# A graph network on one core: both counting sorts made bucket by bucket, source ranks in 40 written-out groups, node loads behind the fill

## The reference

```
h = features @ W_layer.T + b_layer                       # layer 1
v = leaky_relu(a1[row] + a2[col]);  m = segment_max(v, row)
ev = exp(v - m[row])
out = segment_sum(ev / segment_sum(ev, row)[row] * h[col], row)
...
for l in range(3):                                       # layers after the router
    msg = relu(x[src] * (edge_attr @ edge_w + edge_b))
    for i in range(3):                                   # three edge types
        h = segment_sum(msg * (edge_type == i), dst) * inv_cnt[i]
        out = out + h @ weights[l, i]
    out = out + x @ roots[l] + biases[l]
    x = residual + relu(out)
```

## Time and profile before

| | |
|---|---|
| median of the runs | 5961.54 us |
| profiled execution, its own time | 5950.92 us |
| its span | 5949.1 us |
| busy in the span: PE, DVE, ACT, POOL | 75%, 71%, 38%, 69% |
| mean granted TensorE clock | 0.904 |

### The profile page before, as it was taken

How to read it: one execution, slowest core, us unless ns; L and a number is a source line. 1 busy time by engine, 2 the same in 40 slices (tenths; PEclk the granted TensorE clock), 3 DMA queues, 4 the chain that set the end, 5 groups by cost and what they waited for, 6 DMA issues and landing times.

```text
span 5949.1 us, 89553 instructions
## 1 busy us (share of the span) xinstructions
PE 4487.4 (75%) x25082; PEld 2797.4 (47%) x25082; DVE 4196.2 (71%) x9654; ACT 2286.6 (38%) x5880; POOL 4087.5 (69%) x4202
## 2 busy tenths in 40 slices
PE   6459987899888876777777767777776777777787
PEld 2135544666666644444444434444444444444455
DVE  8789986777777654666766757777675777777734
ACT  0038875555555523333333323333332223232321
POOL 1467777777777777777777757777776777777700
PEclk9579998888898888999999989999999999999979
DMA  5011111434333313444444434444444444445400
GB/s 149 19 40 29 29 26 37 108 107 107 106 102 101 93 35 111 135 135 129 133 133 131 134 104 139 139 138 139 139 139 117 137 139 138 140 138 140 137 25 22
DMA packets 445005, 624.93 MB, mean 105 GB/s; under 512 B 97099, under 2 KB 330261, under 8 KB 444564
## 3 DMA queue, kind: packets, MB, share of 16 engines
q0 software_dynamic: 187648, 457.52, 27.7%
q1 hardware_dynamic: 250164, 159.14, 9.5%
q10 hardware_dynamic: 6754, 2.96, 0.2%
HBM read 556.32 MB, written 62.94 MB: 104 GB/s over the span
## 4 chain that ended last, share of the span: by engine, by line
PE 25%; DVE 14%; issue 11%; POOL 10%; ACT 2%; DVEq 2%; DMA 1%; POOLq 0%; ACTq 0%; SPq 0%
PE banks L1173 13%; DVE acc_mem L1692 6%; POOL sort_mem L623 6%; DVE z_mem L1835 5%; PE banks L1203 4%; POOL recB_d L581 3%; PE banks L1161 2%; PE banks L1106 1%; PE banks L1116 1%; DMA sort_mem<-x_d,x_mem 1%; DVEq L1681 1%; DVEq L1692 1%; ACT z_mem L809 1%; PE banks L1158 1%; PE banks L1193 1%
## 5 line engine op out<-in xcount | busy, mean ns | idle before, releaser
L623 POOL DMA_INDIRECT sort_mem<-x_d,x_mem x2568 | 2454.3, 956 | 877.7 <-issue 764.3
L1173 PE MATMUL banks<-z_mem 128*128 128x257 f32 x5136 | 1567.7, 430 | 903.9 <-DVE acc_mem L1692 766.8
L1173 PEld LDWEIGHTS banks<-z_mem 128*128 128x128 f32 x5136 | 850.5, 199 | 1601.3 <-ACT z_mem L809 718.4
L1692 DVE TENSOR_TENSOR acc_mem<-acc_mem,banks 128x257 f32 x2568 | 1081.8, 421 | 556.0 <-PE banks L1173 383.0
L809 ACT ACTIVATE z_mem<-z_mem 128x512 f32<-128x512 f32 x1284 | 768.8, 628 | 1375.6 <-DVE z_mem L1835 1375.6
L1835 DVE TENSOR_TENSOR z_mem<-banks,sort_mem 128x512 f32<-128x512 f32 x1284 | 825.4, 685 | 412.3 <-PE banks L1161 301.6
L581 POOL DMA_INDIRECT recB_d<-acc_mem,sort_mem x680 | 708.6, 1042 | 410.6 <-DVE sort_mem L1423 205.4
L590 POOL DMA_INDIRECT acc_mem<-h_d,xnt_mem x808 | 798.3, 988 | 246.1 <-issue 235.5
L1049 PE MATMUL banks<-acc_mem,xnt_mem 128*128 128x257 f32 x1616 | 579.3, 483 | 44.0 <-DVE acc_mem L1635 41.8
L1635 DVE SCALAR_TENSOR_TENSOR acc_mem<-acc_mem,z_mem,banks 128x257 f32 x808 | 386.7, 479 | 114.8 <-PE banks L1049 100.4
L1161 PE MATMUL banks<-z_mem,x_mem 32*128 32x256 f32 x5136 | 422.1, 404 | 0.0
(11 more groups left out here) (355 smaller groups left out, 5714.1 us busy)
## 6 DMA issues: line engine op xcount, KB each, us to landing
x_mem<-recB_d SPq DMA_DIRECT2D x642, 68.0 KB
sort_mem<-x_d,x_mem POOLq DMA_INDIRECT x2568
x_mem<-at_d SPq DMA_DIRECT2D x428, 64.0 KB
at_d<-x_mem SPq DMA_DIRECT2D x214, 64.0 KB
acc_mem<-h_d,xnt_mem POOLq DMA_INDIRECT x808, 2.8
x_mem<-x_d SPq DMA_DIRECT2D x100, 128.0 KB, 2.5
acc_mem<-in_edge_attr SPq DMA_DIRECT2D x40, 312.5 KB
recB_d<-acc_mem SPq DMA_DIRECT2D x3, 3672.0 KB, 26.1
```

The costliest lines, as they stand in the source:

```text
L623: pool.indirect_dma_start(out=xg[h % XG][:, k, :], out_offset=None, in_=x_ds[l % 2], in_offset=bass.IndirectOffsetOnAxis(ap=reci[h][:, k, ...
L1173: m.matmul(bank[5 + tile % 2][:, :AC], oneh[:, Q % 2, k, :], msg[:, Q % 2, k, :], start=True, stop=True)\
L1692: v.tensor_tensor(a_, a_, bank_[:, :AC], ALU.add).then_inc(flushed, 1)
```

## The change

Four parts. (1) `count` makes one mask of all 800 columns for each bucket (`tensor_scalar` with a constant) and PE adds its two halves of 400 columns to row b of two banks, so that the counts come out as [bucket, column] with no transposes. The masks lie in `held`, 25 slots; sort B goes round them three times, sort A's stay for its ranks. (2) Sort A's ranks are made in 40 groups of 20 columns, written out, with the product of group q ahead of the reduce of q-1; product and matrices are now bucket-major, so the reduce reads them with a step of 20 elements. Late body 3 moves ahead of them. Sort A's base is not turned before it is stored: 25 rows of 800. (3) On SP the load of x and first weights moves from ahead of the fill to behind the loads of late body 1, and POOL makes the fill record and `pick` first, record memsets last. (4) DVE splits only the target ids before sort B; the source's part (`split_ids`) and the items (`make_items`) come later. ACT stores sort B's base before it makes records.

```diff
+        GROUPS_A = EC // 20
+        def mask_slot(b):
+            return held[:EP, b % BKT_A, :]
+        def hot_A(q):
+            return held[:, :, q * 20:(q + 1) * 20]
+        def in_buckets(m_):
+            return m_[:EP, :20 * BKT_A].rearrange("p (b c) -> p b c", b=BKT_A)
+        FILL_MADE, GRID_MADE, ALL_MADE = 5, 13, 15 + len(late_recs)
...
@@ SP
-            x_rows = t["x"][0:(NT - 1) * P, :].rearrange("(t p) d -> p t d", p=P)
-            sp.wait_ge(S("x_zeroed"), 1)
-            sp.dma_start(x_sb[:, 0:NT - 1, :], x_rows).then_inc(S("x_loaded"), 16)
...
+            def load_nodes():
+                x_rows = t["x"][0:(NT - 1) * P, :].rearrange("(t p) d -> p t d", p=P)
+                sp.wait_ge(S("x_zeroed"), 1)
+                sp.dma_start(x_sb[:, 0:NT - 1, :], x_rows).then_inc(S("x_loaded"), 16)
...
-            sp.wait_ge(S("fill_ready"), 1)
+            sp.wait_ge(S("p_const"), FILL_MADE)
...
                 if i + 2 < BODIES:
                     load_attr(i + 2)
+                if i == 1:
+                    load_nodes()
...
@@ ACT
+            store_base_B()
+            act.wait_ge(S("p_const"), ALL_MADE)
             act.wait_ge(S("items_ready"), 1)
-            for i in range(2):
+            for i in range(4):
                 make_records(i)
-            store_base(SORT_B)
-            for i in range(2, 4):
-                make_records(i)
-            store_base(SORT_A)
-            act.dma_start(held[EP:, :], baseA_d).then_inc(S("held_rows"), 16)
+            store_base_A()
...
@@ PE, count
-                            m.matmul(bank[half][:4 * n, :cols * nb], pick[:, ds((i * 4 + k) * -1 + 79, 4 * n)],
...
+                for b in range(nb):
+                    pe.wait_ge(S("onehot"), before + b + 1)
+                    for half in range(2):
+                        last = m.matmul(bank[half][:nb, :EC // 2], pick[:, 79 - b:79 - b + nb],
+                                        mask_slot(b)[:, half * (EC // 2):(half + 1) * (EC // 2)], start=b == 0, stop=b == nb - 1)
+                    last.then_inc(S("counted"), 1)
...
@@ PE, ranks
+            late_body(3)
             pe.wait_ge(S("held_rows"), 16)
+            for q in range(GROUPS_A):
+                if q >= 2:
+                    pe.wait_ge(S("rank_masked"), q - 1)
+                m.matmul(in_buckets(bank[q % 2]), tri_b[:, :EP], hot_A(q), start=True, stop=True).then_inc(S("ranked"), 1)
...
@@ DVE, count
+                for b in range(nb):
+                    if b >= BKT_A:
+                        dve.wait_ge(S("counted"), b - BKT_A + 1)
+                    v.tensor_scalar(mask_slot(b), s["key"], float(b), None, ALU.is_equal).then_inc(S("onehot"), 1)
+                if n_ == 0:
+                    make_items()
+                    dve.wait_ge(S("p_const"), GRID_MADE)
...
@@ DVE, ranks
+            def product_A(q):
+                dve.wait_ge(S("ranked"), q + 1)
+                if q >= 2:
+                    dve.wait_ge(S("rank_summed"), q - 1)
+                v.tensor_tensor(in_buckets(prod[q % 2]), in_buckets(bank[q % 2]), hot_A(q)[:EP], ALU.mult)\
+                    .then_inc(S("rank_masked"), 1)
+            def slots_A(q):
+                dve.wait_ge(S("rank_masked"), q + 1)
+                v.tensor_reduce(slotf[:, q * 20:(q + 1) * 20], in_buckets(prod[q % 2]).rearrange("p b c -> p c b"),
+                                X_AXIS, ALU.add).then_inc(S("rank_summed"), 1)
...
             count(SORT_B)
+            split_ids()
             late_body(0)
             late_body(1)
             count(SORT_A)
             late_body(2)
-            looped_from(dve, 0, SORT_A["bodies"] // 2, rank_A)
             late_body(3)
-            looped_from(dve, SORT_A["bodies"] // 2, SORT_A["bodies"], rank_A)
+            for q in range(GROUPS_A):
+                product_A(q)
+                if q:
+                    slots_A(q - 1)
```

More of the change, by code:

```diff
@@ L127, in looped @@
             body(n - 1)
-        def looped_from(eng, lo, hi, body):
-            body(lo)
-            with eng.Fori(lo + 1, hi - 1) as i:
-                body(i)
-            body(hi - 1)
         x_mem = sb("x_mem", [P, NT * D])
@@ L547, in _ @@
             g.memset(fill, 0.0).then_inc(S("p_const"), 1)
-            g.memset(erec, 0.0).then_inc(S("p_const"), 1)
-            for late in late_recs:
-                g.memset(late, 0.0).then_inc(S("p_const"), 1)
-            g.iota(addrB, pattern=[[1, EC]], base=P * TB - EP * EC, channel_multiplier=EC).then_inc(S("p_const"), 1)
+            g.memset(pick, 0.0).then_inc(S("p_const"), 1)
+            pool.wait_ge(S("p_const"), 2)
+            g.memset(pick[:, 79:80], 1.0).then_inc(S("p_const"), 1)
+            g.memset(fill.rearrange("p (t c) -> p t c", c=RW)[:, :, W_SEG:W_SEG + 1], -1.0).then_inc(S("p_const"), 1)
+            g.iota(fill.bitcast(INT32).rearrange("p (t c) -> p t c", c=RW)[:, :, W_SRC:W_SRC + 1], pattern=[[1, 8], [0, 1]],
+                   base=0, channel_multiplier=24).then_inc(S("p_const"), 1)
             g.iota(iota, pattern=[[1, P]], base=0, channel_multiplier=0,
@@ L873, in _ @@
             m = nc.tensor
-            pe.wait_ge(S("const_ready"), 1)
+            pe.wait_ge(S("p_const"), FILL_MADE)
             def count(s):
-                nb, cols, n_ = s["nb"], s["cols"], s["n"]
-                before = n_ * GROUPS_B
-                for half in range(2):
-                    n = s["bodies"] // 2
-                    def body(i):
-                        for k in range(4):
-                            q = (i + half * n) * 4 + k
-                            pe.wait_ge(S("onehot"), before + q + 1)
-                            if half == 0 and isinstance(i, int) and i == 0 and k == 0 and n_ == 1:
-                                pe.wait_ge(S("counts_read"), 1)
-                            m.matmul(bank[half][:4 * n, :cols * nb], pick[:, ds((i * 4 + k) * -1 + 79, 4 * n)],
-                                     hot(s, k, q)[:EP], start=isinstance(i, int) and i * 4 + k == 0,
-                                     stop=isinstance(i, int) and i * 4 + k == 4 * n - 1).then_inc(S("counted"), 1)
-                    looped(pe, n, body)
-                for half in range(2):
-                    pe.wait_ge(S("rows_copied"), n_ * 2 + half + 1)
-                    G = s["bodies"] * 2
-                    for c in range(cols):
-                        last = m.transpose(bank[2 + half][:nb, c * G:(c + 1) * G], prod[half][:G, c * nb:(c + 1) * nb],
-                                           ident[:G, :G])
-                    last.then_inc(S("counts_turned"), 1)
+                nb, n_ = s["nb"], s["n"]
+                before = n_ * BKT_B
+                if n_:
+                    pe.wait_ge(S("counts_read"), 1)
+                for b in range(nb):
[4 more added lines that the diff above has]
+                    last.then_inc(S("counted"), 1)
+                pe.wait_ge(S("const_ready"), 1)
                 pe.wait_ge(S("tiles_ready"), n_ + 1)
@@ L1262, in _ @@
             st.settle()
[L1263 to L1285 removed]
+            st.run(v.scalar_tensor_tensor(keyB, hi_i, float(R), rel_i, ALU.mult, ALU.add))
@@ new lines, in make_items, with split_ids @@
+            def make_items():
+                st.did(v.tensor_copy(itemB[:, 0, :].bitcast(INT32), src_i))
+                st.run(v.tensor_copy(itemB[:, 1, :], lo_i))
+                dve.sem_inc(S("items_ready"), 1)
+            def split_ids():
+                dve.wait_ge(S("p_const"), ALL_MADE)
+                st.did(v.tensor_single_scalar(hi_i, src_i, 7, ALU.logical_shift_right))
+                st.did(v.tensor_single_scalar(lo_i, src_i, 127, ALU.bitwise_and))
+                st.did(v.tensor_scalar(dstm, dst_i, float(-MID), None, ALU.add))
+                st.settle()
+                st.did(v.tensor_copy(keyA, hi_i))
+                st.did(v.tensor_scalar(segp, lo_i, 1.0, None, ALU.add))
+                st.did(v.tensor_copy(iota_h, iotaT[:, :TA]))
+                st.settle()
```

173 lines of the change are left out of this document (60 added, 113 removed).

## The result

The changed kernel takes 5877.19 us, the median of 4 runs (5873.36 to 5877.75), against 5962.59 of the kernel before beside it (4 runs, 5959.02 to 5966.57): 85.4 us less, a ratio of 0.9854 (95% interval 0.9839 to 0.987). The profiled execution takes 5877.75 with a span of 5875.9; that is 73.2 less than the earlier trace rows; the run of the kernel before that was profiled (5950.92) was 11.7 under the median of the others, and the part on the unchanged kernels says where.

A forecast was written before the change was run, and what follows sets the result against it. POOL was taken to wait for DVE's slot addresses until body 8, then run its own fixed row. Gains 3.7 + 45.3 + 2.1 + 19.8 + 0.8 + 7.9 + 12.3 = 91.9 took 5961.5 to 5869.6 us, range 5846 to 5904.

The forecast's parts named there:

- The mechanism: POOL waits for DVE until body 8's address at 427.94 us; that moves to 336, so the whole 91.9 us passes.
- Ids: DVE from first id split to sort B's first mask: three instructions, 2.15 us instead of 5.9, gain 3.7.
- Sort B's count: Sort B's masks on DVE and matmuls on PE: 29.7 us instead of 75.0, gain 45.3; bounds 27 and 50.7.
- The rival of a low clock throughout: PE stays at low clock in both counts, 50.7 and 17.4 us; gain 65.7, time 5896; chance 0.18.
- Source split hidden behind the base store: The put-off split_ids, some 3.1 us on DVE, is hidden in the 3.62 wait for sort B's base store.
- The fill ends by 60: On SP's queue the fill, issued from about 2.5 us, ends by 60, before the first scatter at 76.5.
- Sort A's count, tail: Sort A's masks and counts 12.2 us instead of 32.0, gain 19.8; its copies, tail and base parts gain 0.8.
- Base rows of sort A: DVE's 7.9 us wait for sort A's base rows is covered by a second late body; gain 7.9, or 6.7.
- Ranks: Sort A's ranks on DVE: 40 groups of 1.66 us, 67.4 instead of 79.7, gain 12.3.
- nothing extra: Rival: the ranks' stepped reads cost nothing, 14.4 us more gain, time 5855; chance 0.10.
- twice the extra: Rival: the ranks' stepped reads cost twice the extra, time 5884; chance 0.07.
- SP: Load of x and weights starts about 74 us, ends by about 97; late body 2's base rows, wanted about 105, stay unaffected.

The follow-up runs named there:

- the part on the unchanged kernels: Kernel before and changed kernel profiled again, unchanged; body 8's address to first gather took 591.1 and 614.5 before, 597.9, 600.2 and 609.7 changed.
- the added 18.7 us: Changed kernel plus 20 unused reduces of 500 f32 elements on DVE ahead of late body 4; median 5907.16 us.
- the further 16.9 and 25.6: Changed kernel with sort A's product in column pairs, 5885.90 us; with pairs, a third product buffer and ten unused PE matmuls before sort A's masks, 5871.27 us.

## Why the prediction was right

5870 was forecast, 5877.19 measured, inside 5846 to 5904; 91.9 of gain forecast, 91.4 at body 8, and 85.4, 101.1 and 93.3 by the medians of three series. The mechanism, that POOL takes over what DVE gains ahead of body 8's address, is borne out for this change by its address wait at 336.57 (forecast 336), by the added 18.7 us, which reached body 8 and the end, and by the phase of scatters behind it, equal in the mean. It is not borne out in full beyond it: of the further 16.9 and 25.6 at body 8 the means show 11.5 and 11.3, uncertain by 6 and 5. Term by term:

- *Ids*: mis-sized, 7.9 for 3.7. "I take no difference" between x and the fill behind the ids was the step: the run with x first put the mask 4.1 back.
- *Sort B's count*: 28.1 for 29.7. PE bound it as worked out, at 0.169 a matmul of 400; the low clock lasted 3.9 us and not 5.8, and a mask then took 0.334 and not 0.35. The rival of a low clock throughout (0.18) did not happen. Gaps were the argument against it: in the kernel before, with 35.12 busy of 40, PE stayed at 530 ns a matmul, and here, without gaps, it rose. The run with added matmuls shows a gap of 4.5 us after which PE was at 1.2 GHz again; that the short gaps of before kept it there is not shown.
- *Source split hidden behind the base store*: hidden, but the store itself grew by 2.6 (10.2 for 7.65), since the fill and the attributes are still in the queues. That term was taken as nothing. "The fill ends by 60" was known; what it does to a store at 55.2 was not asked. It is the term that could have cost most: 13.5 of wait in the other order.
- *Sort A's count, tail*: 20.5 and 0.7 for 19.8 and 0.8.
- *Base rows of sort A*: 7.3 for 7.9, with a second reason that the prediction gave no price: the layout of the store does 6.6 alone, and the late body put ahead of the ranks at most 1.3 on top. Of the 0.6 that is missing, 0.54 is that body's wait for its own base rows.
- *Ranks*: mis-sized, 8.6 for 12.3. The reduce was 1.081 for 1.03, and the product started 0.11 behind it instead of 0.04: 1.785 a group for 1.66. The rivals on the step: nothing extra (5855) and twice the extra (5884) both fell; the nearest row's 0.36 for 500 was 0.35 at its own step and 0.42 at 20.
- *SP*: hidden as forecast, and by more: x and the weights were issued from 69.80 to 83.65, not from 74 to 97.

The misses of +4.2, -2.6 and -3.7 make -2.1 together, and the smaller ones give 1.6 of it back. That the sum came within 0.5 of 91.4 is luck: single terms were off by up to 4.2. The 7.2 between forecast and median need no cause of their own: the same two kernels lay 15.7 and 7.9 further apart in the later series.

## What to carry to other kernels

Where an engine with a fixed row of work waits for addresses, what is gained ahead of the last wait moves all that follows; here the first 91 us arrived in full, of 16.9 and 25.6 more the means show 11 to 12. So take stretches apart by the events in the profile and not by the total. When a stretch is cut short, look at what still fills the DMA queues at the new time: a store that was alone before may now share them. And before accepting a stepped read in f32, try a layout in pairs: a step of 2 was free for the reader and runs of two for the writer, where steps of 4 to 20 cost the reader, and one of 25 the writer, more than half again.

## What the runs showed of the hardware

- DVE, 500 f32: neighbours or a step of 2 take 674 ns, steps of 4, 5 and 20 take 1027, 1040 and 1092; a write stepped by 25 makes a product 1144 where 679 is normal. The cost of reading hardly grows from a step of 4 to one of 20.
- The product, which waits for PE and for the reduce just ahead of it, starts 0.11 us after that reduce ends; when it waits for an older reduce it starts 0.08 to 0.09 before the end. With 40 groups that is 7.5 us. A reduce that waits for the product just ahead alone starts 0.03 after it.
- PE's matmuls went from 537 to 333 ns, 1.2 to 2.4 GHz, 3.9 us after work without gaps began in one place and 4.6 in another; behind a gap of 4.5 us PE was at 1.2 GHz, behind one of 0.55 at 2.4.
- Three stores of 117 KB took 2.08 us to issue on idle queues, 6.03 and 7.15 while the fill (107 x 272 x 128 f32, 14.9 MB) and the attributes were in the queues.
- Indirect scatters of 0.96 us have a tail of some that take 1.6 to 2.6; their number, 6 to 22 in 440, moves a phase of 600 us by 27.
